# One launch of a six-layer local-attention stack: the step that normalises the rotated heads goes ahead of the softmax's maximum, and the rotary tables are scaled first in ScalarE's turn

## The chip, the cores and the metric

The kernel runs on 1 core of one Trainium2 chip. The metric is the device time of one execution in microseconds (us). The kernel before took 1337.75 us (median of 3 runs, 1335.63 to 1342.5).

## What is computed

The input is 2 sequences of 512 tokens with 128 channels. Three blocks follow each other, each closed by a residual and a layer norm: a Mamba block with a mixture of experts, a cross-attention, and a stack of six layers. The stack takes about two thirds of the time and holds the whole change. One of its layers is:

```
def attn_layer(x, Wqkv, qs, ksc, Wo):            # 16 heads of 64, windows of 32
    q, k, v = split(x @ Wqkv)                     # per head
    q = l2norm(q) * qs;  k = l2norm(k) * ksc
    q = q * cos * scale + rotate_half(q) * sin * scale
    k = k * cos / scale + rotate_half(k) * sin / scale
    sim = (q_window @ (this and previous window of k).T) * 8, masked
    return softmax(sim) @ (the same windows of v) @ Wo

for i in range(6):
    x = attn_layer(shift_tokens(x), ...) + x
    x = ffn_layer(shift_tokens(x), ...) + x       # layer norm, W1, a * gelu(gate), W2
```

## The kernel before, in words

**Units and heads.** Channels lie on the 128 partitions and a sequence's 512 tokens along the free dimension. In each layer ("turn") the attention is cut into 16 units, 8 for each of the two sequences; a unit is a pair of heads' worth of scores. The projections run in 16 "heads" h as well: an even h is the q part and an odd h the k part of four real heads. So units n = 2g and 2g + 1 need the steps h = 2g and 2g + 1.

**Passes.** Every engine runs the same loop, `for t in s.range`, whose pass t handles different stages of several units, a software pipeline written out by hand. The turns follow each other without a break, so a layer has 16 passes and pass 16 is pass 0 of the next. In pass t:

- TensorE: the scores of unit t+1 (L1307), the projection of head t+4 in three products of split weights (L1266 to L1270), the transposes of the probabilities of unit t (L1319), the output projection (L1341), v of unit t+1 (L1290), the sum of squares of head t+4 over its partitions (L1278), and probabilities times v of unit t (L1331).
- VectorE (DVE): the maximum over the scores of unit t+1 (L1610), the scores less the maximum (L1616), `normalise_heads` for head t+3 (L1556: the smaller of the reciprocal norm and 1e12, times the rotated head, into `turned`), `rotate` for head t+4 (L1545 and L1546: the projection in PSUM times the sine and cosine tables), and the sum and reciprocal of the softmax (L1640, L1644).
- ScalarE (ACT): the square of head t+4 (L1426), the exponential of unit t+1 (L1489), two copies of the transposed probabilities of unit t (L1457), the copy of v (L1466), logarithm and exponential that give the reciprocal norm of head t+4 (L1433, L1437), and the copy of the attention's output (L1450).
- GpSimd (POOL): the sum of the two squares of head t+4 (L1673), two additions that finish the rotation of head t+4 (L1677, L1678), and the probabilities of unit t+1 times the reciprocal (L1685).
- SyncE: `place_heads` for head t+3: DMAs from `turned` into `qT` (4 of them, for an even head) or into `k_blocks` (8, for an odd head), and then two DMAs that shift v.

Each engine works through its list in order and waits on semaphores. `normalise_heads` of head h waits for POOL's second addition for h and for ACT's reciprocal norm of h, both made in the pass before; the place DMAs wait for it, and the scores of unit 2g wait for the k_blocks of head 2g + 1, which is normalised one pass before those scores.

**Extra work in some passes.** Passes 8 to 11 also carry the feed-forward of the first sequence ("job 0"), passes 0 to 3 that of the second ("job 1", one turn late); these four passes are its stages 0 to 3. In stage 0 DVE adds the attention's output to the stream (`residual1`, L1564), which TensorE's mean (L1345) waits for; then DVE centres (L1580), ACT squares (L1501) and TensorE forms the variance (L1349). In stage 2 DVE forms two gated products (`gated`, L1597), which the v product of TensorE waits for, as it needs the same PSUM bank. In stage 3 DVE adds the result (`residual2`, L1571), ACT writes its high part (L1518) and DVE its low part (L1649) for the next layer's projections. In passes 7 to 14 DVE casts the next layer's weights (`high_weights`, L1536) and POOL forms the rest (L1662), in all layers but the last.

**The rotary tables.** `scale_table` (L1444, two ACT instructions for each of two tables) multiplies the tables by the next layer's scales. It runs in pass 11 for the q table and in pass 12 for the k table, after `product_done` says that the last head that uses the old table has been rotated, that is after the rotation in the pass before.

**Buffers.** `turned` has 4 places, `mx`, `rn` and `prob` have 2, `cos_part` has one for q and one for k; `sin_part` has one. The profile writes `mo_w` for `cos_part` and `pn`, `x` for `sin_part` and `oT`, `h` for the squares.

Of the kernel before, what the change touches and what calls it, by code (L numbers as in the profile page):

```python
# [1085 lines left out]
def build_stack(nc, ctx, Y, places, spare, d, C):  # L1086
# [54 lines left out]
    product_done, add_done = flow("product_done", 2 * UNITS), flow("add_done", 2 * UNITS)  # L1141
# [276 lines left out]
    @block.scalar  # L1418
    def _(ac):
        A = nc.scalar.activation  # L1420

        def square(s, h):
            ac.wait_ge(*qk_done.at(s.turn, h + 1))
            if sq_summed.any(s.turn, h):
                ac.wait_ge(*sq_summed.at(s.turn, h))
            A(sq[:], QK_BANKS, ACT.Square).then_inc(sq_done.sem, 1)  # L1426

        def logarithm(s, h):

            ac.wait_ge(*norm_done.at(s.turn, h + 1))  # L1430
            if rope_done.any(s.turn, h - 1):
                ac.wait_ge(*rope_done.at(s.turn, h - 1))
            A(rn[:, h % 2, :], NORM_BANK, ACT.Ln, bias=C["tiny"], scale=SS_SCALE).then_inc(ln_done.sem, 1)  # L1433

        def root(s, h):
            ac.wait_ge(*ln_done.at(s.turn, h + 1))
            A(rn[:, h % 2, :], rn[:, h % 2, :], ACT.Exp, bias=C["ln_scale"], scale=-0.5).then_inc(r_done.sem, 1)  # L1437

        def scale_table(s, which, ahead):

            ac.wait_ge(*scale_in.at(s.turn, 16 * ahead + 16))
            for part in range(2):
                col = 2 * which + part
                A(scaled[:, which, :, part, :], table[:, 2 * which:2 * which + 2, :], ACT.Copy, scale=rope_scale[:, col:col + 1]).then_inc(scaled_done.sem, 1)  # L1444

        def copy_out(s, n):
            ac.wait_ge(*pv_done.at(s.turn, n + 1))
            if wo_step.any(s.turn, n - 1):
                ac.wait_ge(*wo_step.at(s.turn, n - 1))
            A(oT[:, n % 2, :], TURN_BANK, ACT.Copy).then_inc(o_copied.sem, 1)  # L1450

        def copy_probs(s, n):
            r = n % 2
            ac.wait_ge(*t_done.at(s.turn, n + 1))
            for half in range(2):
                rows = slice(64 * half, 64 * half + 64)
                A(p_blocks[rows, r, half, :], TURN_BANK[rows, :], ACT.Copy).then_inc(pt_copied.sem, 1)  # L1457

        def copy_v(s, n):
            r = n % 2  # L1460
            ac.wait_ge(*v_done.at(s.turn, n + 1))
            if pv_done.any(s.turn, n - 1):
                ac.wait_ge(*pv_done.at(s.turn, n - 1))
            if vs_in[r].any(s.turn, 32 * (n // 2)):
                ac.wait_ge(*vs_in[r].at(s.turn, 32 * (n // 2)))
            A(vn[:, r], V_BANK.rearrange("p (j f) -> p j f", f=P), ACT.Copy).then_inc(v_copied.sem, 1)  # L1466

        def gelu(s, job, j):
            ac.wait_ge(*up_done.at(s.turn, 6 * job + (1, 2, 5)[j]))
            if act_done.any(s.turn, 3 * job + j // 2):  # L1470
                ac.wait_ge(*act_done.at(s.turn, 3 * job + j // 2))
            A(gate[0:ROWS[j], j % 2, :], (V_BANK if j == 1 else OUT_BANK[job % 2])[0:ROWS[j], :], ACT.Gelu, bias=ffn_param[0:ROWS[j], 5 + j:6 + j]).then_inc(gate_done.sem, 1)

        def body(s):
            for t in s.range:
                job, stage = s.stage(t)
                if stage == 1:
                    ac.wait_ge(*stat_done.at(s.turn, 2 * job + 2))
                    if centre_step.any(s.turn, 3 * job):
                        ac.wait_ge(*centre_step.at(s.turn, 3 * job))  # L1480
                    A(rstd[:], OUT_BANK[job % 2], ACT.Ln, bias=C["eps"]).then_inc(rstd_step.sem, 1)
                    ac.wait_ge(*rstd_step.at(s.turn, 3 * job + 2))
                    A(rstd[:], rstd[:], ACT.Exp, scale=-0.5).then_inc(rstd_step.sem, 1)
                if s.unit(t + 4):
                    square(s, t + 4)
                if t >= -1 and s.unit(t + 1):
                    n = t + 1
                    ac.wait_ge(*sub_done.at(s.turn, n + 1))
                    A(prob[:, n % 2], prob[:, n % 2], ACT.Exp, scale=QK_SCALE).then_inc(exp_done.sem, 1)  # L1489
                if s.unit(t) and t >= 0:  # L1490
                    copy_probs(s, t)
                if t >= -1 and s.unit(t + 1):
                    copy_v(s, t + 1)
                if s.unit(t + 4):
                    logarithm(s, t + 4)
                    root(s, t + 4)
                if stage == 0:
                    ac.wait_ge(*centre_step.at(s.turn, 3 * job + 1))
                    if stat_done.any(s.turn, 2 * job):
                        ac.wait_ge(*stat_done.at(s.turn, 2 * job))  # L1500
                    A(dsq[:], dx[:], ACT.Square).then_inc(rstd_step.sem, 1)  # L1501
                if t >= 0 and s.unit(t):
                    copy_out(s, t)
                if stage == 1:
                    ac.wait_ge(*ffn_in.at(s.turn, 80 * (job + 1) if job < 1 else 80))
                    gelu(s, job, 0)
                    gelu(s, job, 1)
                    nc.scalar.preload_act_table_set("natural_log_exp_and_others")
                if stage == 2:
                    gelu(s, job, 2)  # L1510
                    nc.scalar.preload_act_table_set("natural_log_exp_and_others")
                if t in (11, 12) and not s.last:
                    ac.wait_ge(*product_done.at(s.turn, 2 * (t + 4)))
                    scale_table(s, t - 11, 1)
                if s.resplit(job, stage):

                    ac.wait_ge(*res2_done.at(s.turn, 2 * job + 2))
                    A(y_high[:, job % 2, :], Y[:, job % 2, 0:SEQ], ACT.Copy).then_inc(y_high_done.sem, 1)  # L1518

        nc.scalar.preload_act_table_set("natural_log_exp_and_others")  # L1520
        for b in range(2):
            A(y_high[:, b, :], Y[:, b, 0:SEQ], ACT.Copy).then_inc(y_high_done.sem, 1)
        ac.wait_ge(table_in.sem, 16)
        for which in range(2):
            scale_table(Steps(0, True, False), which, 0)
        ac.wait_ge(pads_zero.sem, 3)
        all_turns(ac, body)

    @block.vector
    def _(dv):  # L1530
# [17 lines left out]
        def normalise_heads(s, h):  # L1548

            which, g = h % 2, h // 2  # L1550
            dv.wait_ge(*add_done.at(s.turn, 2 * h + 2))
            dv.wait_ge(*r_done.at(s.turn, h + 1))
            for pair in range(2):
                if heads_in[g % 2][pair].any(s.turn, HEADS_IN * (g // 2)):
                    dv.wait_ge(*heads_in[g % 2][pair].at(s.turn, HEADS_IN * (g // 2)))
            v.scalar_tensor_tensor(turned[:, h % 4], rn[:, h % 2, :].unsqueeze(1).to_broadcast([P, 2, SEQ]), 1e12, cos_part[:, which],  # L1556
                                   ALU.min, ALU.mult).then_inc(rope_done.sem, 1)
# [42 lines left out]
        def body(s):  # L1600
            for t in s.range:
                job, stage = s.stage(t)
                n = t + 1
                if t >= -1 and s.unit(n):
                    r = n % 2
                    bank = SCORE_BANK.rearrange("p (i k) -> p i k", k=64)
                    dv.wait_ge(*score_done.at(s.turn, n + 1))
                    if sub_done.any(s.turn, n - 1):
                        dv.wait_ge(*sub_done.at(s.turn, n - 1))
                    v.tensor_reduce(mx[:, r, :], bank, AX, ALU.max).then_inc(mx_done.sem, 1)  # L1610
                    dv.wait_ge(*mx_done.at(s.turn, n + 1))
                    if pn_done.any(s.turn, n - 1):
                        dv.wait_ge(*pn_done.at(s.turn, n - 1))
                    if sum_done.any(s.turn, n - 1):
                        dv.wait_ge(*sum_done.at(s.turn, n - 1))
                    v.tensor_tensor(prob[:, r], bank, mx[:, r, :].unsqueeze(2).to_broadcast([P, 8, 64]), ALU.subtract).then_inc(sub_done.sem, 1)  # L1616
                if stage == 0:
                    residual1(s, job)
                if t >= -3 and s.unit(t + 3):
                    normalise_heads(s, t + 3)  # L1620
                if s.first and t + 5 < PARTS:
                    high_weights(s, t + 5, 0)
                if t >= PARTS - 1 and t < 2 * PARTS - 1 and not s.last:
# [295 lines left out]
```

## Time and profile before

| | us |
|---|---|
| median of 3 runs | 1337.75 |
| lowest, highest | 1335.63, 1342.5 |
| the profiled execution | 1334.07 |
| its span in the profile | 1332.3 |

| engine | busy us | share |
|---|---|---|
| PE (matmul) | 1143.7 | 86% |
| DVE | 951.0 | 71% |
| ACT | 834.3 | 63% |
| POOL | 671.2 | 50% |

The share is the part of the span in which the engine had an instruction in execution; a matmul's end is modelled. The stack runs from about 390 to 1310 us. TensorE's mean granted clock is 0.954 of full speed over the span, and 0.99 to 1.00 in the stack's layers.

### The profile page before, as it was taken

Reading aid. Unit: us, or ns where it says so; the run is one execution under the profiler, and the core shown is the slowest. Engines: PE = TensorE matmul, PEld = TensorE weight load, DVE = VectorE, ACT = ScalarE, POOL = GpSimd, SP = SyncE. Lnnn points to the kernel's source line nnn. Section 1 sums busy time; section 2 is a strip of 40 time slices with the busy share of each in tenths; the row PEclk is TensorE's granted clock in tenths of the full one; section 3 lists DMA queues with packets and bytes.
Section 4 is the critical chain, followed back from the end, with each engine's and each line's share of the span. In section 5 each row is a group of like instructions: output and inputs, shape, how many; then the busy total and the mean of one; then the engine's idle time right before and its main releaser. Section 6 shows DMA issues by size and latency. Waiting matters only on the chain. (4 is left out here: it accounts for less than half of the span.)

```text
span 1332.3 us, 25833 instructions
## 1 busy us (share of the span) xinstructions
PE 1143.7 (86%) x9541; PEld 716.3 (54%) x9636; DVE 951.0 (71%) x1207; ACT 834.3 (63%) x1260; POOL 671.2 (50%) x522
## 2 busy tenths in 40 slices
PE   7787879998656898998988998899989989899975
PEld 2222347776224665656555655656555655566541
DVE  2798957776646787877877787867877786877733
ACT  4553446665354667776776767676767667676834
POOL 1555524443326665755655465755555555645510
PEclk9888969999878999999999999999999999999987
DMA  3000035100203443445334442444333532434310
GB/s 108 1 0 0 1 49 198 48 24 1 95 1 79 128 111 77 108 103 132 80 92 105 116 111 72 110 115 121 78 92 102 134 96 69 108 91 110 87 46 16
DMA packets 75507, 107.08 MB, mean 80 GB/s; under 512 B 25347, under 2 KB 31938, under 8 KB 75002
## 3 DMA queue, kind: packets, MB, share of 16 engines
q1 hardware_dynamic: 75386, 105.47, 30.3%
q8 instruction: 76, 1.25, 0.4%
q14 instruction: 45, 0.37, 0.1%
HBM read 30.89 MB, written 0.59 MB: 24 GB/s over the span
## 5 line engine op out<-in xcount | busy, mean ns | idle before, releaser
L1673 POOL TENSOR_TENSOR st_sq_sum<-h 128x512 f32<-128x512 f32 x96 | 130.1, 1355 | 201.4 <-ACT h L1426 201.4
L1677 POOL TENSOR_TENSOR mo_w<-mo_w,x 128x512 f32<-128x512 f32 x96 | 122.3, 1274 | 154.0 <-DVE mo_w L1546 154.0
L1426 ACT ACTIVATE h<-banks 128x1024 f32<-128x1024 f32 x96 | 98.3, 1024 | 144.1 <-PE banks L1270 143.8
L1610 DVE TENSOR_REDUCE st_mx<-banks 128x8 f32<-128x512 f32 x96 | 66.4, 692 | 165.6 <-PE banks L1307 165.2
L1278 PE MATMUL banks<-st_sq_sum,head_ones 128*128 128x512 f32 x192 | 106.6, 637 | 47.9 <-POOL st_sq_sum L1673 46.6
L1556 DVE SCALAR_TENSOR_TENSOR st_turned<-st_rn,mo_w 128x1024 f32<-128x1024 f32 x96 | 124.3, 1295 | 5.9 <-POOL mo_w L1678 5.5
L1545 DVE TENSOR_TENSOR x<-banks,st_scaled 128x1024 f32<-128x1024 f32 x96 | 117.0, 1218 | 15.4 <-ACT h L1426 14.0
L1290 PEld LDWEIGHTS banks<-st_wv,stream 128*128 128x128 f32 x768 | 100.7, 192 | 49.7 <-issue 49.3
L1678 POOL TENSOR_TENSOR mo_w<-mo_w,x 128x512 f32<-128x512 f32 x96 | 122.5, 1276 | 0.0
L1307 PE MATMUL banks<-st_k_blocks,st_qT 128*32 128x128 f32 x3072 | 105.5, 279 | 16.9 <-DMA st_k_blocks<-st_turned 16.9
L1331 PEld LDWEIGHTS banks<-st_p_blocks,st_vs 128*64 128x64 f32 x1536 | 77.8, 137 | 74.2 <-issue 72.9
L1546 DVE TENSOR_TENSOR mo_w<-banks,st_scaled 128x1024 f32<-128x1024 f32 x96 | 116.4, 1213 | 0.0
L1457 ACT ACTIVATE st_p_blocks<-banks 64x512 f32<-64x512 f32 x192 | 112.3, 585 | 3.5 <-PE banks L1319 1.1
L430 POOL TENSOR_TENSOR ma_dbx<-ma_u,ma_b_rows 128x1024 f32<-128x1024 f32 x32 | 75.4, 2360 | 76.1 <-ACT ma_b_rows L288 51.9
L1266 PE MATMUL banks<-st_y_high,st_w_high 128*128 128x512 f32 x192 | 91.9, 479 | 21.2 <-issue 11.6
L1685 POOL TENSOR_TENSOR mo_w<-st_prob,st_ri 128x512 f32<-128x512 f32 x96 | 100.3, 1045 | 17.9 <-DVE st_ri L1644 17.9
L1290 PE MATMUL banks<-st_wv,stream 128*128 128x128 f32 x768 | 102.4, 277 | 0.8 <-issue 0.8
L1433 ACT ACTIVATE st_rn<-banks,fill 128x512 f32<-128x512 f32 x96 | 66.0, 688 | 58.9 <-PE banks L1278 58.9
L1341 PE MATMUL banks<-x,st_wo 128*128 128x512 f32 x192 | 101.7, 612 | 0.9 <-ACT x L1450 0.8
L1331 PE MATMUL banks<-st_p_blocks,st_vs 128*64 128x64 f32 x1536 | 99.4, 228 | 2.8 <-ACT st_p_blocks L1457 2.1
L1307 PEld LDWEIGHTS banks<-st_k_blocks,st_qT 128*32 128x32 f32 x3072 | 79.1, 111 | 41.5 <-DMA st_k_blocks<-st_turned 23.1
L1331 PE MATMUL banks<-st_p_blocks,st_vn 128*64 128x64 f32 x1536 | 94.8, 222 | 0.0
(230 smaller groups left out, 2629.2 us busy)
## 6 DMA issues: line engine op xcount, KB each, us to landing
st_qT<-st_turned SPq DMA_DIRECT2D x192, 128.0 KB, 2.4
st_k_blocks<-st_turned SPq DMA_DIRECT2D x384, 64.0 KB, 2.0
st_vs<-st_vn SPq DMA_DIRECT2D x96, 192.0 KB, 2.5
st_w_raw<-in_w_qk SPq DMA_DIRECT2D x12, 512.0 KB, 4.7
st_vs<-st_vn SPq DMA_DIRECT2D x96, 48.0 KB, 2.1
mo_w_all<-gate_rows SPq DMA_DIRECT2D x1, 3072.0 KB, 12.9
st_wv<-in_w_v SPq DMA_DIRECT2D x12, 256.0 KB, 3.0
st_wo<-in_wo SPq DMA_DIRECT2D x12, 256.0 KB, 3.1
```

The source lines that it names most:

```text
L1278: mm(NORM_BANK, C["head_ones"], sq_sum[:], start=True, stop=True).then_inc(norm_done.sem, 1)
L1290: last = mm(V_BANK[:, rows], Y[:, b, rows], wv[:, pair, :], start=True, stop=True)
L1307: last = mm(SCORE_BANK[rows].rearrange("p (o h i k) -> p o h i k", o=2, h=2, i=2)[:, odd, :, i, :], qT[:, r, pair, t0:t0 + WIN], k_blocks[ ...
L1331: last = mm(TURN_BANK[rows, P * j:P * j + P].rearrange("p (h o q) -> p h o q", h=2, q=WIN)[:, :, odd, :], (vn if odd else vs)[:, r, j, row ...
L1341: mm(OUT_BANK[b], wo[:, pair, :], oT[:, n % 2, :], start=(pair == 0), stop=(pair == 7)).then_inc(wo_step.sem, 1)
L1457: A(p_blocks[rows, r, half, :], TURN_BANK[rows, :], ACT.Copy).then_inc(pt_copied.sem, 1)
L1545: v.tensor_tensor(sin_part[:], QK_BANKS, scaled[:, which, 1], ALU.mult).then_inc(product_done.sem, 1)
L1546: v.tensor_tensor(cos_part[:, which], QK_BANKS, scaled[:, which, 0], ALU.mult).then_inc(product_done.sem, 1)
L1556: v.scalar_tensor_tensor(turned[:, h % 4], rn[:, h % 2, :].unsqueeze(1).to_broadcast([P, 2, SEQ]), 1e12, cos_part[:, which], ALU.min, ALU. ...
L1673: nc.gpsimd.tensor_tensor(sq_sum[:], sq[:, 0, :], sq[:, 1, :], ALU.add).then_inc(sq_summed.sem, 1)
L1677: nc.gpsimd.tensor_tensor(cos_part[:, which, 0, :], cos_part[:, which, 0, :], sin_part[:, 1, :], ALU.subtract).then_inc(add_done.sem, 1)
L1678: nc.gpsimd.tensor_tensor(cos_part[:, which, 1, :], cos_part[:, which, 1, :], sin_part[:, 0, :], ALU.add).then_inc(add_done.sem, 1)
```

## The change

DVE calls `normalise_heads(s, t + 3)` as the first thing in a pass, ahead of the maximum, and no longer after `residual1`. ACT calls `scale_table` at the start of passes 11 and 12, ahead of everything else in the pass, and no longer near their end. The instructions themselves, what they wait for and their buffers are the same.

```
@@ ScalarE
         def body(s):
             for t in s.range:
                 job, stage = s.stage(t)
+                if t in (11, 12) and not s.last:
+                    ac.wait_ge(*product_done.at(s.turn, 2 * (t + 4)))
+                    scale_table(s, t - 11, 1)
                 if stage == 1:
                     ac.wait_ge(*stat_done.at(s.turn, 2 * job + 2))
...
                     nc.scalar.preload_act_table_set("natural_log_exp_and_others")
-                if t in (11, 12) and not s.last:
-                    ac.wait_ge(*product_done.at(s.turn, 2 * (t + 4)))
-                    scale_table(s, t - 11, 1)
                 if s.resplit(job, stage):
@@ VectorE
                 n = t + 1
+                if t >= -3 and s.unit(t + 3):
+                    normalise_heads(s, t + 3)
                 if t >= -1 and s.unit(n):
...
                     v.tensor_tensor(prob[:, r], bank, mx[:, r, :].unsqueeze(2).to_broadcast([P, 8, 64]), ALU.subtract).then_inc(sub_done.sem, 1)
                 if stage == 0:
                     residual1(s, job)
-                if t >= -3 and s.unit(t + 3):
-                    normalise_heads(s, t + 3)
                 if s.first and t + 5 < PARTS:
                     high_weights(s, t + 5, 0)
```

## Rows read from the trace of the kernel before

**Rows 1.** Waits in the stack, 400:1300; us in total, times, longest.
```profile
DVE st_mx L1610 <- PE banks L1307: 165.2, 85, 6.0
PE banks L1307 <- DMA st_k_blocks<-st_turned: 16.9, 18, 2.9
```

**Rows 2.** Timeline of PE: scores of passes 4, 5, 7, 8; start us, us.
```profile
750.40 1.08 PE L1307 MATMUL banks<-st_k_blocks,st_qT 128*32 128x128 f32 x32
758.88 1.08 PE L1307 MATMUL banks<-st_k_blocks,st_qT 128*32 128x128 f32 x32 [0.55 <-DMA st_k_blocks<-st_turned]
...
773.76 1.08 PE L1307 MATMUL banks<-st_k_blocks,st_qT 128*32 128x128 f32 x32 [0.25 <-DMA st_k_blocks<-st_turned]
781.05 1.08 PE L1307 MATMUL banks<-st_k_blocks,st_qT 128*32 128x128 f32 x32
```

**Rows 3.** Timeline of DVE in pass 6, a plain pass.
```profile
767.31 0.69 DVE L1610 TENSOR_REDUCE st_mx<-banks 128x8 f32<-128x512 f32 x1 [1.48 <-PE banks L1307]
768.04 0.69 DVE L1616 TENSOR_TENSOR st_prob<-banks,st_mx 128x512 f32<-128x512 f32 x1
768.65 1.22 DVE L1556 SCALAR_TENSOR_TENSOR st_turned<-st_rn,mo_w 128x1024 f32<-128x1024 f32 x1
769.93 1.23 DVE L1545 TENSOR_TENSOR x<-banks,st_scaled 128x1024 f32<-128x1024 f32 x1
```

**Rows 4.** Timeline of POOL, the end of the same pass.
```profile
772.37 1.28 POOL L1677 TENSOR_TENSOR mo_w<-mo_w,x 128x512 f32<-128x512 f32 x1 [1.11 <-DVE mo_w L1546]
773.60 1.29 POOL L1678 TENSOR_TENSOR mo_w<-mo_w,x 128x512 f32<-128x512 f32 x1
```

**Rows 5.** Timeline of DVE and of POOL in pass 14 of the first layer.
```profile
546.08 2.05 DVE L1556 SCALAR_TENSOR_TENSOR st_turned<-st_rn,mo_w 128x1024 f32<-128x1024 f32 x1 [0.29 <-POOL mo_w L1678]
...
546.00 1.04 POOL L1685 TENSOR_TENSOR mo_w<-st_prob,st_ri 128x512 f32<-128x512 f32 x1
```

**Rows 6.** Timeline of ACT and of PE in pass 6.
```profile
769.79 0.62 ACT L1489 ACTIVATE st_prob<-st_prob 128x512 f32<-128x512 f32 x1
770.32 1.20 ACT L1457 ACTIVATE st_p_blocks<-banks 64x512 f32<-64x512 f32 x2
...
771.31 1.13 PE L1278 MATMUL banks<-st_sq_sum,head_ones 128*128 128x512 f32 x2 [0.26 <-POOL st_sq_sum L1673]
```

**Rows 7.** Timeline of DVE and of PE in a stage 0 (pass 8).
```profile
635.32 1.40 DVE L1564 TENSOR_TENSOR stream<-banks,stream 64x512 f32<-64x512 f32 x2
...
636.77 1.13 PE L1345 MATMUL banks<-stream,mean_ones 128*128 128x512 f32 x2
...
639.15 1.12 PE L1278 MATMUL banks<-st_sq_sum,head_ones 128*128 128x512 f32 x2 [0.37 <-POOL st_sq_sum L1673]
```

**Rows 8.** Timeline of DVE and POOL in passes 8 and 10, PE in pass 10.
```profile
637.89 1.36 DVE L1536 CAST st_w_high<-st_w_raw 128x256 fp32r<-128x256 f32 x1
...
637.55 1.54 POOL L1673 TENSOR_TENSOR st_sq_sum<-h 128x512 f32<-128x512 f32 x1 [1.56 <-ACT h L1426]
...
654.52 0.69 DVE L1610 TENSOR_REDUCE st_mx<-banks 128x8 f32<-128x512 f32 x1 [1.36 <-PE banks L1307]
...
657.73 1.40 DVE L1597 SCALAR_TENSOR_TENSOR st_act<-banks,st_ffn_param,st_gate 128x512 f32<-128x512 f32 x2
...
658.03 1.27 POOL L1673 TENSOR_TENSOR st_sq_sum<-h 128x512 f32<-128x512 f32 x1 [0.36 <-ACT h L1426]
...
659.23 1.13 PE L1290 MATMUL banks<-st_wv,stream 128*128 128x128 f32 x8 [0.17 <-issue]
```

**Rows 9.** Timeline of ACT in passes 11 and 12.
```profile
667.33 1.02 ACT L1426 ACTIVATE h<-banks 128x1024 f32<-128x1024 f32 x1
...
675.08 2.17 ACT L1444 ACTIVATE st_scaled<-st_table,st_rope_scale 128x1024 f32<-128x1024 f32 x2
677.16 0.62 ACT L1518 ACTIVATE st_y_high<-stream 128x512 fp32r<-128x512 f32 x1
680.66 1.02 ACT L1426 ACTIVATE h<-banks 128x1024 f32<-128x1024 f32 x1 [2.89 <-PE banks L1270]
```

More of the change, by code:

```diff
@@ L1476, in body @@
                 job, stage = s.stage(t)
+                if t in (11, 12) and not s.last:
+                    ac.wait_ge(*product_done.at(s.turn, 2 * (t + 4)))
+                    scale_table(s, t - 11, 1)
                 if stage == 1:
@@ L1511, in body @@
                     nc.scalar.preload_act_table_set("natural_log_exp_and_others")
-                if t in (11, 12) and not s.last:
-                    ac.wait_ge(*product_done.at(s.turn, 2 * (t + 4)))
-                    scale_table(s, t - 11, 1)
                 if s.resplit(job, stage):
@@ L1603, in body @@
                 n = t + 1
+                if t >= -3 and s.unit(t + 3):
+                    normalise_heads(s, t + 3)
                 if t >= -1 and s.unit(n):
@@ L1618, in body @@
                     residual1(s, job)
-                if t >= -3 and s.unit(t + 3):
-                    normalise_heads(s, t + 3)
                 if s.first and t + 5 < PARTS:
```

## The prediction

> **What bounds the kernel now.** I read the waits of the stack first. DVE waits longest of all for TensorE's scores, 165.2 us in 85 passes [rows 1]: the maximum stands first in its pass, and all that follows on DVE stands behind it. TensorE has few waits; one is for the k blocks, whose DMA follows `normalise_heads`: 16.9 us in 18 passes [rows 1]. Then I took a stretch of plain passes (no feed-forward). From pass 7 to pass 8 the scores start 7.29 us apart; the four passes 4 to 7 take 30.65 us, 0.80 of it in waits for k blocks [rows 2]. Third, DVE and POOL side by side. In pass 6 the scores end at 767.24; DVE takes the maximum at 767.31, subtracts, normalises from 768.65 (end +2.63, counted from the scores' end), rotates from 769.93, and POOL adds until 774.89 [rows 3, 4]. The next scores end at 774.84 [rows 2]. So the next head can be normalised at about the time at which the next scores are there, within 0.1 us here; where no DMA wait stretched the pass it is 0.35 later than they (7.65 after the scores' end against a pass of 7.29). This is the number on which the case turns: the change puts an instruction that is ready late ahead of one that is ready early.
>
> **The ring that the change closes.** Before, the ring between DVE and POOL was: second addition, normalise, rotate, additions; the maximum stood outside it, in DVE's idle time. After, it is second addition, normalise, maximum, subtract, rotate twice, two additions. From rows, start to start: normalise to maximum (its duration less 0.08, as L1556 starts 0.08 before the end of L1616), maximum to subtract 0.73, subtract to the next 0.61, first product to first addition 2.44 (769.93 to 772.37, the second product between), to the second addition 1.23, its length 1.29, and 0.04 to the normalisation [rows 3, 4]. The last is 0.08, the head start that POOL's product has in rows 5, less the 0.04 by which POOL starts an instruction before the end of the last (773.60 against 772.37 + 1.28). Without the normalisation the ring is 6.34. With 1.22 less 0.08 it is 7.5, just over the pass of 7.29.
>
> But the normalisation will not take 1.22. Released by the second addition, it starts together with POOL's next instruction, the probabilities' product (L1685). The trace has one pass in which exactly this happened, released by L1678: POOL's product ran from 546.00 to 547.04, and the normalisation from 546.08 took 2.05, which is the product's end plus 1.09 [rows 5]. Before, it started 1.40 after the scores, mostly when that product was over. After, it starts with the addition's end in nearly every pass, so I take 2.05, and the ring takes 1.97 + 6.34 = 8.3 us. The other end is 1.22, if that one row were chance.
>
> The Trainium skill has a rule that speaks against this change: "SBUF — State Buffer", section "Who interferes with whom", says that a DVE instruction with two SBUF inputs and a GpSimd instruction that reads SBUF take turns at a shared port pair as at an exclusive lock, and that whoever issues first keeps it. By that rule the normalisation (two SBUF inputs) waits the product out in each pass, and the ring is the 8.3 above; without it, 7.5. The row agrees with the rule.
>
> **Plain passes.** Where does TensorE stand in a pass of the ring? The subtraction ends 3.39 after the normalisation starts (1.97 + 0.73 + 0.69), the exponential and the two copies take 0.04 + 0.62 - 0.10 + 1.20 = 1.76 [rows 6], and from the start of probabilities times v to the end of the next scores it is 2.15 (774.84 less the wait of 0.25, less the norm's end at 772.44) [rows 2, 6]. Together 7.4, so in the steady state the scores end 7.4 after the last normalisation started, and the next one starts 0.9 after them. Pass 4 begins with a reset (the feed-forward leaves slack): by the same recurrence passes 4 to 7 take 7.9 + 7.8 + 8.3 + 8.3 = 32.3 against 30.65 - 0.80 = 29.85 without DMA waits: +2.5, in five layers 12.5. Passes 12 to 15, started in the same way, +2.4 in five layers: 12. The first layer's first eight passes have no feed-forward, but their pass is longer by itself (7.8): +4.9. Against it goes what the change is good for: for k heads the normalisation ends at +1.2 to +3.0 instead of +2.6 relative to the scores, but relative to the next scores always early enough, and the 16.9 us of waits for k blocks [rows 1] fall to about 2: -15. Sum of the plain passes: +14.
>
> **Stage 0, eleven times with heads to normalise.** Here `residual1` moves from before the normalisation to behind it, and TensorE's mean waits for it. Before, residual1 ends at 636.72, which is 0.07 + 0.73 + 0.61 + 1.40 = 2.81 after the scores' end, and the mean starts 0.05 later, just in time [rows 3, 7]. After, with the normalisation starting at +1.1 in pass 8 (the ring's lag, and 0.25 for the weight cast that pass 7 adds): + 1.97 + 0.73 + 0.61 + 1.40 = 5.8. The mean is 3.0 late. Behind it in TensorE's queue stand v and the norm's sum; the norm had waited 0.37 for POOL, so it is 2.6 late, and logarithm, root, square and variance, all in a row after it, pass this on whole. Six times 2.6; in pass 0 of the five later layers the lag is 0.9: 2.4 each. Sum +27.6. The low end, if the ring has no lag and the normalisation 1.22: in pass 8 it starts at +0.4, the mean is 1.5 late, the norm 1.1; 0.8 in pass 0: about +11.
>
> **Stage 2.** The weight cast L1536 stretches to the end of POOL's sum of squares when both meet: 637.89 for 1.36 against a sum that ends at 639.09 [rows 8]. In pass 10 DVE reaches the cast after subtraction, at 3.8 after the scores, and the sum runs from 3.58 (658.03 less the scores' end, 0.07 before the maximum's 654.52) [rows 8]. So the cast ends at about 5.1, the two gated products (1.40) at 6.6 instead of 4.68, and the v product, which starts at 4.78 now, waits 1.85 [rows 8]. Five layers: +9.3. In pass 2 there is no cast: +0.3, six times, 1.8. If the cast comes before the sum, this term is 1 to 2 instead of 11. Stage 1 gains about 0.2, five times: -1; in stage 3 DVE waits for ACT's square anyway: 0.
>
> **The tables.** In pass 11 ACT is late already: the square starts at 667.33 with no idle time before it [rows 9]. Two instructions of 2.17 together ahead of it delay square, sum, norm, down product and residual2 by 2.1. But they leave the place at 675.08 ahead of the high part L1518 [rows 9], which then starts as early as residual2 allows: 2.1 earlier in its place, so at the same time as before. Zero, between -1 and +1 in all; if pass 12 did not give it back, +11 (5 x 2.17). In pass 12 they lie in the 2.89 us in which ACT waits for the projection [rows 9], and the 0.2 that they cost pass 13 goes: -1.
>
> **Sum.** 14 + 27.6 + 11.1 - 1 - 1 = 50.7, say 50. On the profiled execution's own time, 1334.07 (span 1332.3, 1.8 around it), this gives 1384 us. The median of the runs shown, 1337.75, lies 3.7 above that execution; I keep to the profiled one and let the range take this up.
>
> **The rivals.**
> - *Faster: the normalisation is free in DVE's idle time.* The 165 us of idle before the maximum [rows 1] take it in, k blocks arrive early (-15), the rotation starts sooner in the feed-forward's passes. 1334 - 16 = 1318. It decides for this if POOL's second addition ends at least 1.2 (better 2.0) before the scores. In plain passes it ends after them [rows 2, 4]; in passes 1 to 4 and 11 it ends before. Chance 0.05.
> - *No lock.* One row is not a law; with 1.22 the ring is 7.5, plain passes come to -10 net, stage 0 to +13, the rest to 0: 1334 + 3 = 1337. Chance 0.08.
> - *Only stage 0 pays.* The mean's wait is real (+20), but the ring's lag is soaked up by slack that I don't see, and the cast comes before the sum: 14 becomes 0 and 11 becomes 2: about 1356. Chance 0.15.
> - *The tables cost.* All of the forecast, and 2.17 in pass 11 is not given back: 1395. For it, ACT's lateness there; against it, that L1518 waits behind the tables today. Chance 0.07.
>
> **How the numbers follow.** My forecast has 0.65; its own range is 1362 to 1400, by stage 2's term between 2 and 11 and half of the plain passes' gross loss either way. The range for 8 in 10 reaches down over the stage 0 rival: 1348 to 1402. A run can tell 0.5% (6.7 us) from no change. Faster by more: the first rival, 0.05. Within: the second and a little of the third, 0.08. Slower: 0.87.
>
> **What would show it.** In the changed kernel's trace: L1556's mean near 2.0 us instead of 1.3, its release by POOL L1678; the maximum following L1556 and no longer waiting for scores in plain passes; scores 8.3 us apart in passes 5 to 7; TensorE idle 3 us before the mean L1345, eleven times, released by L1564; the wait for k blocks nearly gone; the v product in pass 10 waiting for L1597 by 1.8; ACT's square in pass 11 2.1 late and L1518 at the same distance from pass 10 as before. The prediction is wrong if L1556 stays near 1.2 us (then the ring fits the pass), or if the mean does not wait.

## The result, and the profile after

| | before | after |
|---|---|---|
| median, us | 1336.69 | 1398.59 |
| lowest to highest | 1333.53 to 1342.5 | 1396.51 to 1402.52 |
| span of the profiled execution | 1332.3 | 1394.7 |
| TensorE's mean granted clock | 0.954 | 0.943 |

The changed kernel is slower: ratio 1.046, 95% interval 1.043 to 1.049, 62 us. The forecast was 1384 in a range of 1348 to 1402.

The page of the changed kernel, busy time by engine:

```profile
PE 1185.6 (85%) x9636; PEld 725.0 (52%) x9636; DVE 1001.2 (72%) x1207; ACT 836.9 (60%) x1260; POOL 684.0 (49%) x522
```

No instruction was added, but DVE is busy for 50 us more. The groups by line (busy us, mean ns, idle before), DVE in the stack, say which line it is:

```profile
L1556 DVE SCALAR_TENSOR_TENSOR st_turned<-st_rn,mo_w 128x1024 f32<-128x1024 f32 x96 | 185.0, 1927 | 156.2 <-POOL mo_w L1678 150.7 <-ACT st_rn L1437 5.4
L1612 DVE TENSOR_REDUCE st_mx<-banks 128x8 f32<-128x512 f32 x96 | 65.3, 680 | 6.2 <-PE banks L1307 5.9
```

`normalise_heads` (L1556) takes 1.93 us in the mean instead of 1.30 (185.0 us in all instead of 124.3), and DVE's idle time has moved. Before, 165 us of it lay ahead of the maximum, until the scores came [rows 1]; now 151 us lie ahead of L1556, until POOL's second addition. DVE waits in another place, behind which the maximum now stands. The maximum is L1612 in this kernel.

The waits of the stack (us in total, times, longest), those that the forecast named:

```profile
PE banks L1345 <- DVE stream L1564: 28.9, 12, 2.6
PE banks L1319 <- POOL mo_w L1685: 18.4, 28, 1.2
PE banks L1331 <- ACT st_p_blocks L1457: 18.2, 37, 1.5
PE banks L1307 <- DMA st_k_blocks<-st_turned: 0.9, 3, 0.4
```

The wait for k blocks, 16.9 us before [rows 1], is gone. TensorE's mean waits for residual1 instead, and in plain passes the transposes wait for POOL's product and the values for ACT's copies: the DVE and POOL ring seen from TensorE.

The ring itself, DVE and then POOL in passes 5 and 6 of the same layer as in rows 3 (cut at `...`):

```profile
786.07 2.05 DVE L1556 SCALAR_TENSOR_TENSOR st_turned<-st_rn,mo_w 128x1024 f32<-128x1024 f32 x1 [1.80 <-POOL mo_w L1678]
788.05 0.68 DVE L1612 TENSOR_REDUCE st_mx<-banks 128x8 f32<-128x512 f32 x1
788.76 0.69 DVE L1618 TENSOR_TENSOR st_prob<-banks,st_mx 128x512 f32<-128x512 f32 x1
789.37 1.21 DVE L1545 TENSOR_TENSOR x<-banks,st_scaled 128x1024 f32<-128x1024 f32 x1
...
794.34 2.05 DVE L1556 SCALAR_TENSOR_TENSOR st_turned<-st_rn,mo_w 128x1024 f32<-128x1024 f32 x1 [1.80 <-POOL mo_w L1678]
...
791.79 1.28 POOL L1677 TENSOR_TENSOR mo_w<-mo_w,x 128x512 f32<-128x512 f32 x1 [2.25 <-DVE mo_w L1546]
793.03 1.28 POOL L1678 TENSOR_TENSOR mo_w<-mo_w,x 128x512 f32<-128x512 f32 x1
794.27 1.04 POOL L1685 TENSOR_TENSOR mo_w<-st_prob,st_ri 128x512 f32<-128x512 f32 x1
```

From one L1556 to the next it is 8.27 us. Each is released by L1678 (773.60 + 1.29 in rows 4, here 793.03 + 1.28) and starts 0.07 after L1685; it ends 1.08 after that product's end, as in rows 5. The scores, which came 7.29 us apart in rows 2, come 8.27 apart (passes 6 to 8):

```profile
792.43 1.08 PE L1307 MATMUL banks<-st_k_blocks,st_qT 128*32 128x128 f32 x32
800.71 1.08 PE L1307 MATMUL banks<-st_k_blocks,st_qT 128*32 128x128 f32 x32
808.98 1.08 PE L1307 MATMUL banks<-st_k_blocks,st_qT 128*32 128x128 f32 x32
```

Stage 0 in pass 8, TensorE, to be held against rows 7:

```profile
812.66 0.60 PE L1319 MATMUL banks<-ident,mo_w 128*128 128x128 f32 x4
815.83 1.12 PE L1345 MATMUL banks<-stream,mean_ones 128*128 128x512 f32 x2 [2.57 <-DVE stream L1564]
816.79 1.68 PE L1290 MATMUL banks<-st_wv,stream 128*128 128x128 f32 x8
818.26 0.64 PE L1296 MATMUL banks<-mask,ident 128*128 128x512 bf16 x1
818.68 1.91 PE L1278 MATMUL banks<-st_sq_sum,head_ones 128*128 128x512 f32 x2
```

The mean starts 5.77 after the scores' end at 810.06; the forecast said 5.8. But what follows was not in it. The v product (L1290) takes 1.68 us (1.05 in the filled kernel further down) and the norm 1.91 where it took 1.12 [rows 7]. The granted clock (third column from the end) in stretches of that time, 817.0:820.6 in pass 8, and 850.8:852.8 in pass 11, where TensorE had waited 2.23 us for POOL's sum:

```profile
817.00:820.60 3.60, 3.60 (x13) 1.95 (x13) 3.57 (x5) 0.60 (x1) 0.58 (x1) 0.53 0.39 92
850.80:852.80 2.00, 1.87 (x3) 0.84 (x4) 1.92 (x3) 0.94 (x2) 0.88 (x2) 0.59 0.00 0
```

A mean of 0.53 or 0.59 says that TensorE had the lower of its two levels, 1.2 instead of 2.4 GHz, for most of the stretch; the same place in the kernel before (785.0:788.5) shows 1.00. The clock fell in nine of the eleven passes of stage 0 in which heads are normalised, in all five passes 11 whose tables are scaled, and in the first layer's pass 0, behind a wait of 1.84 us.

**Where the 62 us lie.** The time from the end of one pass's scores to the end of the next's, worked out from the PE rows of each trace. Each number is a median over layers: the second to the sixth in passes 0 to 7, all six in passes 8 to 10, and from pass 11 on the first five, which scale tables for a next layer.

| pass | before | after | DVE half (b1) | stage 0 as before (b2) | filled (b3) | small product (b4) |
|---|---|---|---|---|---|---|
| 0 (stage 0) | 10.56 | 14.50 | 12.85 | 10.57 | 12.84 | 12.09 |
| 1 | 9.53 | 9.18 | 9.51 | 9.38 | 9.73 | 9.17 |
| 2 | 9.52 | 9.93 | 9.93 | 9.93 | 9.93 | 9.52 |
| 3 | 11.16 | 11.17 | 11.17 | 11.17 | 11.17 | 11.16 |
| 4 | 9.29 | 7.82 | 7.82 | 7.81 | 7.81 | 7.81 |
| 5 | 7.28 | 7.98 | 7.99 | 7.99 | 7.99 | 7.28 |
| 6 | 7.66 | 8.28 | 8.28 | 8.34 | 8.27 | 8.27 |
| 7 | 7.28 | 8.27 | 8.27 | 8.21 | 8.27 | 7.29 |
| 8 (stage 0) | 10.55 | 14.57 | 14.70 | 10.57 | 13.04 | 12.24 |
| 9 | 9.99 | 9.19 | 9.32 | 9.98 | 9.71 | 9.19 |
| 10 (stage 2) | 9.93 | 9.53 | 9.53 | 11.56 | 11.56 | 9.51 |
| 11 | 11.17 | 14.93 | 11.17 | 13.23 | 13.24 | 14.69 |
| 12 | 10.98 | 7.81 | 11.17 | 7.82 | 7.82 | 7.82 |
| 13 | 7.53 | 9.23 | 7.80 | 9.23 | 9.23 | 8.48 |
| 14 | 8.40 | 8.92 | 8.93 | 8.93 | 8.93 | 8.17 |
| 15 | 7.72 | 8.93 | 8.92 | 8.92 | 8.92 | 8.17 |

Summed over all layers, before against after: stage 0 +40.9 (eleven times), passes 13 to 15 +13.9, passes 4 to 7 +5.9, the first layer's pass 0 +3.0, passes 11 and 12 together +0.1 (+3.2 in the five layers that scale tables, -3.1 in pass 12 of the last layer, which scales none), the rest -0.9: 63.0 before rounding.

### The profile page after: what moved, and what is told of

Its sections match the earlier page's. It is cut to its first block and busy times, and to the rows that moved or that the text cites. A ratio compares the mean times of both kernels' runs of the same rounds, so it can differ in the third digit from the quotient of the medians.

```text
span 1394.7 us, 25928 instructions
## 1 busy us (share of the span) xinstructions
PE 1185.6 (85%) x9636; PEld 725.0 (52%) x9636; DVE 1001.2 (72%) x1207; ACT 836.9 (60%) x1260; POOL 684.0 (49%) x522
## 5 line engine op out<-in xcount | busy, mean ns | idle before, releaser
L1556 DVE SCALAR_TENSOR_TENSOR st_turned<-st_rn,mo_w 128x1024 f32<-128x1024 f32 x96 | 185.0, 1927 | 156.2 <-POOL mo_w L1678 150.7
L1673 POOL TENSOR_TENSOR st_sq_sum<-h 128x512 f32<-128x512 f32 x96 | 122.3, 1274 | 183.6 <-ACT h L1426 183.6
L1278 PE MATMUL banks<-st_sq_sum,head_ones 128*128 128x512 f32 x192 | 113.5, 675 | 29.2 <-POOL st_sq_sum L1673 26.5
L1290 PEld LDWEIGHTS banks<-st_wv,stream 128*128 128x128 f32 x768 | 105.7, 202 | 58.2 <-issue 58.0
L1331 PEld LDWEIGHTS banks<-st_p_blocks,st_vs 128*64 128x64 f32 x1536 | 82.3, 138 | 95.1 <-issue 92.5
L1678 POOL TENSOR_TENSOR mo_w<-mo_w,x 128x512 f32<-128x512 f32 x96 | 122.6, 1277 | 0.0
L1290 PE MATMUL banks<-st_wv,stream 128*128 128x128 f32 x768 | 108.7, 288 | 5.1 <-issue 4.7
L1492 ACT ACTIVATE st_prob<-st_prob 128x512 f32<-128x512 f32 x96 | 60.3, 628 | 82.6 <-DVE st_prob L1618 82.6
L1685 POOL TENSOR_TENSOR mo_w<-st_prob,st_ri 128x512 f32<-128x512 f32 x96 | 100.2, 1043 | 14.1 <-DVE st_ri L1644 14.1
```

The lines of the kernel that those rows point to most:

```text
L1278: mm(NORM_BANK, C["head_ones"], sq_sum[:], start=True, stop=True).then_inc(norm_done.sem, 1)
L1290: last = mm(V_BANK[:, rows], Y[:, b, rows], wv[:, pair, :], start=True, stop=True)
L1331: last = mm(TURN_BANK[rows, P * j:P * j + P].rearrange("p (h o q) -> p h o q", h=2, q=WIN)[:, :, odd, :], (vn if odd else vs)[:, r, j, row ...
L1673: nc.gpsimd.tensor_tensor(sq_sum[:], sq[:, 0, :], sq[:, 1, :], ALU.add).then_inc(sq_summed.sem, 1)
L1678: nc.gpsimd.tensor_tensor(cos_part[:, which, 1, :], cos_part[:, which, 1, :], sin_part[:, 0, :], ALU.add).then_inc(add_done.sem, 1)
L1685: nc.gpsimd.tensor_tensor(pn[:, r], prob[:, r], ri[:, r, :].unsqueeze(2).to_broadcast([P, 8, 64]), ALU.mult).then_inc(pn_done.sem, 1)
```

## The experiments

Four kernels were run beside the kernel before in each of two groups, two in a third and one last. In the first group the kernel before took 1337.63 us, in the second 1338.58, in the third 1337.91, with the last run 1336.33.

### The DVE half alone (b1)

Against the kernel before, cut at `...`:

```
+                if t >= -3 and s.unit(t + 3):
+                    normalise_heads(s, t + 3)
                 if t >= -1 and s.unit(n):
...
                     residual1(s, job)
-                if t >= -3 and s.unit(t + 3):
-                    normalise_heads(s, t + 3)
```

> The DVE half of the change alone: normalise_heads first in every pass, tables scaled where they were. Mine: the tables are nearly neutral, since what pass 11 loses pass 12 gets back; only the slow clock after the 2.2 us wait in pass 11 is lost with them (about 1.6 us), less about 1 us of gain, five times. So 1395 us (1390 to 1399), passes 11 and 12 together 22.1 instead of 22.7 us. Rival 'the tables cost': pass 11 is 3.7 us longer in the changed kernel and that is a loss of its own, so 1398.6 - 18 = 1380.

Measured 1389.42 us, ratio to before 1.040 (1.036 to 1.043). Neither number was hit: with the tables moved as well it is 9 us slower. Passes 11 and 12 together are 22.24 against 22.79 us (means over the five layers), near what I expected, so 'the tables cost' by pass 11 alone is wrong. Most of the rest is in pass 13, 7.70 instead of 9.14 in the mean: POOL's second addition ends within 0.5 us of the scores when pass 13 begins, and in the changed kernel 1.3 to 1.8 us after them. In pass 0 TensorE kept its clock in three layers of five (12.84 to 12.85 against 14.5), but passes 1 and 2 took 3.3 of those 4.8 us back.

### Stage 0 in the old order (b2)

Against the changed kernel, as are the edits of b3 and b4:

```
-                if t >= -3 and s.unit(t + 3):
+                if t >= -3 and s.unit(t + 3) and stage != 0:
                     normalise_heads(s, t + 3)
...
                 if stage == 0:
                     residual1(s, job)
+                    if s.unit(t + 3):
+                        normalise_heads(s, t + 3)
```

> The changed kernel, but in stage 0 (passes 0 and 8) normalise_heads stands behind residual1 again. Mine: the mean no longer waits, stage 0 goes back from 14.6 to 10.6 us eleven times (-41), but the pass after it then starts with a late normalisation: pass 9 about +1.5 and pass 10 about +1.9 five times (+17). So 1375 us (1366 to 1382). Rival 'the ring alone': the time is lost in the ring of DVE and POOL and stage 0 only shows it, so nearly nothing comes back: 1393 or more.

Measured 1359.86 us, 1.018 (1.014 to 1.023): 39 of the 62 us come back: by the traces 41 in the eleven passes and 8 in pass 11, less 11 in passes 1, 2, 9 and 10. 'The ring alone' is out. Stage 0 went back to 10.57 as expected. Pass 10 rose to 11.56 as expected (+2.0), pass 9 by 0.8, not by 1.5; and pass 11 fell from 14.93 to 13.23, which I had not counted: it kept its clock (1.00), although TensorE's wait there was 2.35 us against 2.23 in the changed kernel. So the length of one wait does not decide; what does, no run here isolates.

### TensorE kept busy in its idle time (b3)

```
+        def filler(s, h, count):
+            if ln_done.any(s.turn, h):
+                pe.wait_ge(*ln_done.at(s.turn, h))
+            for _ in range(count):
+                mm(NORM_BANK, C["head_ones"], table[:, 0, :], start=True, stop=True)
...
                 if stage == 0:
+                    if s.unit(t + 4):
+                        filler(s, t + 4, 2)
                     mean(s, job)
                 if t >= -1 and s.unit(t + 1):
                     project_v(s, t + 1, job, stage)
+                if t == 11 and not s.last:
+                    filler(s, t + 4, 2)
```

> The changed kernel with two more matrix products (head_ones times a rotary table, result never read, into the norm's bank) ahead of the mean in stage 0 and two ahead of the norm in pass 11, where TensorE stands idle for 2.2 to 2.6 us. They take about 2.2 us of that idle time. Theory clock: the products after the idle time run at the lower granted clock (0.53 in 817.0:820.6), 1.5 us in each of 11 stage 0 passes and 1.6 in five passes 11; kept busy, TensorE keeps its clock, so 1398.6 - 24 = 1374 us (1368 to 1380). Rival 'contention': v and the norm are slow there because of what else reads SBUF, and then the time stays at 1398, or goes up by what the products don't fit in.

Measured 1389.95 us, 1.039 (1.036 to 1.043), with more work than the changed kernel and 8.6 us less time. TensorE in pass 8 (the two added products are L1284 at 813.66; mean, v and norm are L1351, L1296, L1278), and the clock in 817.0:820.6:

```profile
813.66 1.88 PE L1284 MATMUL banks<-st_table,head_ones 128*128 128x512 f32 x4
816.40 1.13 PE L1351 MATMUL banks<-stream,mean_ones 128*128 128x512 f32 x2 [0.85 <-DVE stream L1574]
817.36 1.05 PE L1296 MATMUL banks<-st_wv,stream 128*128 128x128 f32 x8
818.47 1.02 PE L1278 MATMUL banks<-st_sq_sum,head_ones 128*128 128x512 f32 x2
```

```profile
817.00:820.60 3.60, 3.52 (x44) 2.40 (x43) 3.04 (x4) 1.64 (x3) 0.01 (x1) 1.00 0.42 102
```

The mean is as late as ever, but v and norm are back to 1.05 and 1.02 us. So their slowness was the clock, and 'contention' is out: apart from the two added products nothing that runs there had changed. Stage 0 takes 12.8 to 13.3 us in every layer and pass 11 13.24 in all but the last. That is 1.5 to 1.7 us less in each of the 14 places in which the changed kernel had lost its clock there, 23.0 us in all, but the total fell by 9 and not by 24. Most of the difference is in pass 10: 11.56 us in each of five layers, which in the changed kernel was 11.56 in two and 9.52 in three. The two are the layers whose pass 8 had kept its clock. A shorter stage 0 lets less slack through to the passes behind it: passes 1, 2, 9 and 10 together take 11.6 us back.

### The lock: POOL's product on an eighth (b4), and its control (c1)

```
-                    nc.gpsimd.tensor_tensor(pn[:, r], prob[:, r], ri[:, r, :].unsqueeze(2).to_broadcast([P, 8, 64]), ALU.mult).then_inc(pn_done.sem, 1)
+                    nc.gpsimd.tensor_tensor(pn[:, r, 0:1], prob[:, r, 0:1], ri[:, r, 0:1].unsqueeze(2).to_broadcast([P, 1, 64]), ALU.mult).then_inc(pn_done.sem, 1)
```

The control has the same edit in the kernel before. Both leave out seven eighths of the product.

> The changed kernel, POOL's probabilities' product L1685 on 64 of its 512 columns (the rest of the probabilities is left as it was in the buffer; this part of the computation is left out). Theory lock: the normalisation waits for that product to end; now it ends in about 0.2 us, L1556 falls from 1.93 to about 1.3 us, the ring from 8.3 to 7.5: plain passes -26, stage 0's mean earlier by 1.4 (-16) and with a wait short enough to keep the clock (-16), so 1340 us (1330 to 1355). Rival 'no lock': L1556 is slow because it starts right after the addition that writes its input, whatever POOL does next: L1556 stays at 1.9 us and the time above 1390.

> Control to the run with the small product: the kernel before, POOL's L1685 on 64 of its 512 columns (the same part left out). In the kernel before the normalisation mostly starts after that product, so both theories of the lock say nearly nothing: 1333 to 1338 us. If it fell to 1300 or lower, the small product would save time by another way and the run of the changed kernel with it would show nothing of the lock.

Measured 1343.09 us, 1.005 (1.002 to 1.007), and for the control 1330.74, 0.995 (0.993 to 0.997). So the small product saves 55 us in the changed kernel and 7 in the kernel before. DVE and POOL in the changed kernel with it:

```profile
776.42 1.30 DVE L1556 SCALAR_TENSOR_TENSOR st_turned<-st_rn,mo_w 128x1024 f32<-128x1024 f32 x1 [1.82 <-POOL mo_w L1678]
783.93 1.30 DVE L1556 SCALAR_TENSOR_TENSOR st_turned<-st_rn,mo_w 128x1024 f32<-128x1024 f32 x1 [1.80 <-POOL mo_w L1678]
...
775.09 1.29 POOL L1678 TENSOR_TENSOR mo_w<-mo_w,x 128x512 f32<-128x512 f32 x1
776.33 0.30 POOL L1685 TENSOR_TENSOR mo_w<-st_prob,st_ri 128x64 f32<-128x64 f32 x1
```

L1556 still starts 0.09 after the product and still ends 1.09 after its end: 776.63 + 1.09 = 777.72. It is short because the product is, so 'no lock' is out, and the ring is 7.51 us (forecast 7.5). What remains against the control, 12 us by the medians, lies by the traces (whose executions are 21 us apart) in stage 0, +19.6 us (1.5 us over 10.56 in pass 0, 1.1 to 4.2 in pass 8), and in passes 11 to 15 of the first five layers, +9.4, where the clock fell in three passes 11; the other passes are 11 us shorter. The control took 2 us less than its range; its saving is its own, and only the 48 us beyond it speak for the lock.

### The cast behind the gated products (c2)

This is b3 with one more edit, cut at `...`:

```
-                if t >= PARTS - 1 and t < 2 * PARTS - 1 and not s.last:
+                if t >= PARTS - 1 and t < 2 * PARTS - 1 and not s.last and stage != 2:
                     high_weights(s, t - PARTS + 1, 1)
...
                 if stage == 2:
                     gated(s, job, 0)
                     gated(s, job, 1)
+                    if t >= PARTS - 1 and not s.last:
+                        high_weights(s, t - PARTS + 1, 1)
```

> The changed kernel with the filling products, and in stage 2 DVE casts the weights (L1536) behind the two gated products and no longer ahead of them. With the filling alone pass 10 came to 11.56 us, against 9.53 without it. Theory cast: DVE reaches the cast while POOL's sum of squares runs, holds it until the sum ends, and TensorE's v product waits for the gated products behind it; without the cast ahead pass 10 falls to about 9.9 us, five times, so 1390 - 8 = 1382 us (1379 to 1385). Rival: the normalisation's lateness alone makes the gated products late, pass 10 stays above 11 and the time at 1390.

Measured 1385.27 us, 1.036 (1.034 to 1.038), 4.7 less than with the filling alone. DVE in pass 10, without this edit and with it (subtract, cast, gated; line numbers of each kernel):

```profile
836.54 0.69 DVE L1628 TENSOR_TENSOR st_prob<-banks,st_mx 128x512 f32<-128x512 f32 x1
837.15 1.19 DVE L1546 CAST st_w_high<-st_w_raw 128x256 fp32r<-128x256 f32 x1
838.27 1.40 DVE L1607 SCALAR_TENSOR_TENSOR st_act<-banks,st_ffn_param,st_gate 128x512 f32<-128x512 f32 x2
```

```profile
834.31 0.69 DVE L1628 TENSOR_TENSOR st_prob<-banks,st_mx 128x512 f32<-128x512 f32 x1
834.92 1.40 DVE L1607 SCALAR_TENSOR_TENSOR st_act<-banks,st_ffn_param,st_gate 128x512 f32<-128x512 f32 x2
836.24 0.28 DVE L1546 CAST st_w_high<-st_w_raw 128x256 fp32r<-128x256 f32 x1
```

Pass 10 is 10.44 us: 1.1 of the 2.0 us were the cast's stretch (1.19 instead of 0.28 while POOL's sum runs), the other 0.9 stay with the late normalisation. Both theories had half: the 4.7 us saved lie between the 8 of the one and the nothing of the other.

### The tables alone (a1)

> The ACT half alone: tables first in passes 11 and 12, DVE as before. Mine: pass 11 +2.2 for the norm's wait and +1.6 for the slow clock after it, pass 12 about -3.1: together +0.3 to +0.7 five times, so 1340 us (1336 to 1344). Rival 'the tables cost': +3.7 in pass 11 stays, 1355.

Its diff is the ScalarE half of the change. Measured 1340.63 us, 1.003 (1.000 to 1.006). The two numbers were 15 us apart and 'mine' was hit: alone, this half loses 2 us, and by the interval between 0.5 and 7.4. By pass it was less near. Pass 11 went from 11.17 to 14.77 and pass 12 from 10.98 to 8.55, together 1.6 us more in the mean of five layers where I had 0.3 to 0.7; the profiled execution, 1345.31, is one of the longer ones.

### What the experiments pointed to (a2, a3, a4, d1)

In pass 4 alone (and 12) POOL's addition ends well before the scores, 2.2 us in each of the later layers; there the early normalisation can be had for nothing. And the tables need not be ahead of `y_high`. The edits are against the kernel before, cut at `...`:

```
+                if t % 8 == 4 and s.unit(t + 3):                       # a2, a4, d1: VectorE, first in the pass
+                    normalise_heads(s, t + 3)
...
-                if t >= -3 and s.unit(t + 3):
+                if t >= -3 and t % 8 != 4 and s.unit(t + 3):           # at its old place in the others
                     normalise_heads(s, t + 3)
```

```
+                if t in (12, 13) and not s.last:                       # a3, a4, d1: ScalarE, first in the pass
+                    ac.wait_ge(*product_done.at(s.turn, 2 * (t + 3)))
+                    scale_table(s, t - 12, 1)
...
-                if t in (11, 12) and not s.last:
-                    ac.wait_ge(*product_done.at(s.turn, 2 * (t + 4)))
-                    scale_table(s, t - 11, 1)
```

```
-                if t >= PARTS - 1 and t < 2 * PARTS - 1 and not s.last:
+                if t >= PARTS - 1 and t < 12 and not s.last:
                     high_weights(s, t - PARTS + 1, 1)
...
+                if t >= 12 and t < 2 * PARTS - 1 and not s.last:       # d1: VectorE, behind rotate in passes 12 to 14
+                    high_weights(s, t - PARTS + 1, 1)
```

> The kernel before, with normalise_heads ahead of the maximum in passes 4 and 12 alone, where the second addition ended 2.2 us before the scores. The k blocks go out 1.4 us earlier there: pass 4 from 8.5-9.9 to 7.8-8.0 us (five layers), pass 12 unchanged: 1337 - 6.5 = 1330 us (1327 to 1334). Rival: the next wait takes its place, 1337.

> The kernel before, with the tables scaled first in ACT's passes 12 and 13 (q table in 12, k table in 13; the heads that use the old ones have long been rotated). In pass 12 they fall into the 2.9 us in which ACT waits for the projection, and no longer stand ahead of the high part that TensorE waits for: -2.1 us five times, 1337 - 10 = 1327 us (1324 to 1331). Rival: the projection then waits for DVE or the weights instead, 1337.

> Passes 4 and 12 as in the run before last and the tables late. Mine: the two add up, 1337 - 17 = 1320 us (1316 to 1326). Rival: in pass 12 they share the same gain, 1327.

> The version with normalise_heads first in passes 4 and 12 and the tables late (1313 us), and in passes 12 to 14 DVE casts the weights (L1536) behind the rotation and no longer ahead of it. In that version the cast of pass 12 meets POOL's sum of squares and takes 1.3 us, the rotation starts at 4.6 us after the scores with its square ready at 3.2, and pass 13 takes 8.98 us instead of 7.5. Mine: pass 13 falls to about 7.7, pass 14 stays or gets its wait for k blocks back in part: -1.2 us five times, 1313 - 5 = 1308 us (1304 to 1313). Rival: the cast behind the rotation holds up POOL's additions by as much, 1313 or more.

| | us | ratio to before | interval |
|---|---|---|---|
| first in passes 4 and 12 (a2) | 1327.0 | 0.992 | 0.990 to 0.995 |
| late tables (a3) | 1327.39 | 0.992 | 0.989 to 0.995 |
| both (a4) | 1313.35 | 0.982 | 0.979 to 0.986 |
| both, cast late (d1) | 1308.6 | 0.980 | 0.976 to 0.984 |

All four are faster. The first three fell as far as expected or further, by 11.6, 11.2 and 25.2 us (a4 came 2.7 us below its range); pass 4 is at 7.81 in a2, passes 11 and 12 together at 20.3 in a3 and 18.99 in a4 instead of 22.1 (means over five layers). Each part has its own gain. In a2 pass 12 of the last layer, which has neither tables nor casts, fell as well, from 9.40 to 6.25, where I had expected no change in pass 12. In d1 pass 13 fell from 8.98 to 7.71 as expected; against a4 the medians differ by 4.7 us, but the intervals of the two overlap, so that the last edit helped is shown by the pass and not by the total. ACT in passes 11 and 12 of a3:

```profile
823.82 0.62 ACT L1518 ACTIVATE st_y_high<-stream 128x512 fp32r<-128x512 f32 x1
824.34 2.18 ACT L1444 ACTIVATE st_scaled<-st_table,st_rope_scale 128x1024 f32<-128x1024 f32 x2
826.45 1.03 ACT L1426 ACTIVATE h<-banks 128x1024 f32<-128x1024 f32 x1
```

The high part, which stood behind the tables in rows 9, stands ahead of them, and they take the time in which ACT waited 2.89 us for the projection.

## Why the prediction was right, and where its sizes were off

**The ring and the lock: right.** L1556 at 2.05 us and a ring of 8.3 were forecast from one row [rows 5], and 8.27 came. The run with the small product separates the lock from the order: 7.51 against a forecast of 7.5. The stall for k blocks fell from 16.9 to 0.9 us where I said 2. Pass 4 to 7 came to 7.82, 7.98, 8.28, 8.27, together 32.35 against 32.3 forecast. One sum has a slip: 3.39 + 1.76 + 2.15 is 7.3 and not 7.4, but 7.45 was measured (794.34 to 801.79), so nothing hangs on it. Passes 13 to 15 take 27.1 us against 23.6 before; pass 12 is 3.2 shorter in exchange and starts them off with less slack, which I had not worked out for the two together. I had also taken their ring for the 8.3 of passes 4 to 7. It is 8.92, because the weight cast is in it and meets POOL's sum of squares (DVE and POOL, pass 14):

```profile
876.94 2.05 DVE L1556 SCALAR_TENSOR_TENSOR st_turned<-st_rn,mo_w 128x1024 f32<-128x1024 f32 x1 [1.81 <-POOL mo_w L1678]
...
880.23 0.72 DVE L1536 CAST st_w_high<-st_w_raw 128x256 fp32r<-128x256 f32 x1
...
885.86 2.05 DVE L1556 SCALAR_TENSOR_TENSOR st_turned<-st_rn,mo_w 128x1024 f32<-128x1024 f32 x1 [1.82 <-POOL mo_w L1678]
...
879.53 1.26 POOL L1673 TENSOR_TENSOR st_sq_sum<-h 128x512 f32<-128x512 f32 x1
```

The cast takes 0.72 us instead of 0.28 and adds 0.64 to the ring (880.23 to 880.87).

**Stage 0: right in place, too small.** The mean at 5.8 was right to 0.03 us. The term was 27.6 and measured 40.9. In the passes in which TensorE kept its clock it is as forecast (13.05 and 13.11 us in pass 8 of two layers of the changed kernel, 10.55 + 2.6 forecast), and with the clock kept everywhere (b3) the term measures 26.4. In the other nine passes it is 1.5 to 1.7 more.

**The missing term: TensorE's clock.** The step that failed is "logarithm, root, square and variance, all in a row after it, pass this on whole": it passes on a wait of 2.57 us and, with it, products at half the clock. It costs 1.5 to 1.7 us in nine passes of stage 0 and five passes 11, 23 us before anything is given back. The trace shows 0.53 granted in 817.0:820.6, and the filled kernel 1.00 in the same stretch. The Trainium skill has the rule, "TensorE: Matmul & The Clock Gate", section "HAM oscillation — how this bites in real kernels": idle time between bursts of products throws the clock back. The waits in the example that the Trainium skill gives there are 3 to 5 us long. The trace agrees with the rule and goes beyond the example: here waits of 2.1 to 2.6 us did it, in 14 places of 16. I had forecast TensorE's idle time before the mean and put down no price for the products behind it.

**Stage 2: right as a mechanism, nearly absent in the sum.** I forecast +9.3 in pass 10. The changed kernel shows it in two layers of five (11.56 us, forecast 9.93 + 1.85), and in three pass 10 is 0.4 shorter than before. What failed is where DVE stands in pass 10, "at 3.8 after the scores": the slow clock makes stage 0 longer, so the ring's lag is gone by then. With the clock kept (b3) all five layers show 11.56, and DVE reaches the cast 3.80 after the scores. So this is the same missing term once more and no error of its own.

**The sum without the missing term.** Set the forecast's groups beside the kernel whose clock was kept (b3) and the changed kernel, each less the kernel before, from the traces:

| us | forecast | b3 | changed |
|---|---|---|---|
| stage 0, eleven passes | 27.6 | 26.4 | 40.9 |
| passes 1, 2, 3, 9, 10 with a feed-forward (11.1 less 1) | 10.1 | 10.4 | -1.1 |
| plain passes and pass 11 (14 less 1 for the tables) | 13 | 15.0 | 23.2 |
| sum | 50.7 | 51.8 | 63.0 |

The forecast describes a kernel that keeps its clock, nearly group by group. The clock adds 14.5 and 8.2 us and takes 11.5 back, 11 us net by the traces and 8.6 by the medians of b3 and the changed kernel. That the total stayed in the range owes something to this: half of the missing term paid itself back, which I had not foreseen.

**The tables: right but for the clock.** I put them between -1 and +1, and the changed kernel is 9 us slower with them than without (b1). Over passes 11 to 15 of five layers the two traces differ by 9.3 us: +18.6 in pass 11, -15.9 in pass 12, +7.2 in pass 13, -0.6 behind it. With the clock kept (b3) pass 11 loses 10.4 and not 18.6, and the same passes are 1.2 us longer than in b1. So what pass 11 waits is given back, near the forecast; what the clock takes there, 8.2 us, is not.

**The rivals.** 'Faster' needed the addition 1.2 us before the scores; in passes 4 and 12, where it ends 2.2 before them, it is right (a2: 11.6 us faster). 'No lock' and 'only stage 0 pays' are out by b4 and by passes 5 to 7. 'The tables cost' hit the total better than my forecast, 1395 against 1398.6, and its price of 11 is near the 9 measured, but for a wrong reason: it was the clock in pass 11 that was not given back.

## What to carry to other kernels

Before an instruction is moved ahead of another on an in-order engine, compare when each is ready: what is ready late drags everything behind it into its own loop of dependences, and that loop's length, not the engine's idle time, sets the pass. The same move can pay in one pass and cost in the next, so decide it pass by pass. A long wait on TensorE (2.2 and 2.6 us here) should be priced with the slower products after it, and that price with what the next stages give back.

## What the runs showed of the hardware that I had not expected

- TensorE's clock fell to its lower level after 2.23 and 2.57 us without a product: v took 1.68 instead of 1.05 us, the norm 1.91 instead of 1.12. It did not fall each time. Two passes 8 of the same kernel kept it behind waits of 2.57 and 2.64 us, and all five passes 11 of b2 behind 2.35 us. What decides is not shown.
- Products whose result nobody reads made the kernel 8.6 us faster, by keeping the clock through a wait that stayed.
- L1556 ends 1.08 to 1.09 us after POOL's product whether this takes 1.04 or 0.30 us. The weight cast, 0.28 us by itself, ends 0.16 after POOL's sum of squares where the two meet (880.95 against 880.79).
